# A windowed-attention block and a gated FFN on one core: another start, scales made on GpSimd, identity products ahead of the first FFN, and a new order of steps

## What is computed

```python
x = x + layernorm(attn(layernorm(x)))
x = x + layernorm(ffn(layernorm(x)))
```

```python
gate = silu((x @ w_gate) * s_gate)
up   = (x @ w_up) * s_up
out  = ((gate * up) @ w_down) * s_down
```

## Time and profile before

| quantity | value |
|---|---|
| median of 3 runs | 1000.24 us (999.96 to 1001.12) |
| the profiled execution's own time | 1001.03 us |
| its span, first to last instruction | 999.3 us |
| busy share of PE, DVE, POOL, ACT | 91%, 83%, 77%, 66% |
| mean granted TensorE clock | 0.968 of 2.4 GHz |

### The profile page before, as it was taken

How to read it: one execution, slowest core, us unless ns; L and a number is a source line. 1 busy time by engine, 2 the same in 40 slices (tenths; PEclk the granted TensorE clock), 3 DMA queues, 4 the chain that set the end, 5 groups by cost and what they waited for, 6 DMA issues and landing times.

```text
span 999.3 us, 17730 instructions
## 1 busy us (share of the span) xinstructions
PE 910.1 (91%) x6511; PEld 705.6 (71%) x6511; DVE 825.5 (83%) x1099; ACT 658.6 (66%) x1153; POOL 765.8 (77%) x698
## 2 busy tenths in 40 slices
PE   1566499989999999999999999999999999989996
PEld 1444387767878777777777787877777787767674
DVE  2799898978898998989898998989898989894322
ACT  1876477676768768586767778586767686654431
POOL 1477686978889797989889797988899787876432
PEclk9878599999999999999999999999999999989998
DMA  7112212040311313040402213040403111120201
GB/s 202 42 43 50 76 26 60 1 128 1 87 41 44 85 22 106 1 127 1 98 30 62 66 33 95 2 128 1 127 1 77 31 43 43 23 64 19 67 11 32
DMA packets 68886, 54.94 MB, mean 55 GB/s; under 512 B 40384, under 2 KB 56768, under 8 KB 68800
## 3 DMA queue, kind: packets, MB, share of 16 engines
q1 hardware_dynamic: 63936, 53.49, 20.0%
q10 hardware_dynamic: 4864, 0.32, 0.3%
HBM read 37.02 MB, written 16.78 MB: 54 GB/s over the span
## 4 chain that ended last, share of the span: by engine, by line
PE 76%; DVE 10%; POOL 5%; issue 3%; DMA 2%; ACT 2%; SPq 1%; POOLq 0%; DVEq 0%; ACTq 0%
PE ps_up L552 21%; PE ps_gate L552 19%; PE ps_acc L571 18%; PE ps_w L513 10%; PE ps_w L533 3%; PE ps_w L504 2%; POOL sum L808 2%; DVE fst L1033 2%; DVE xr L1028 2%; PE ps_w L543 2%; DVE prod L950 1%; PE ps_w L522 1%; DMA xrow<-in_L_attn_x 1%; DVE mid L1049 1%; SPq L432 1%
## 5 line engine op out<-in xcount | busy, mean ns | idle before, releaser
L808 POOL TENSOR_TENSOR sum<-prod 128x1024 f32<-128x1024 f32 x128 | 301.7, 2366 | 46.4 <-DVE prod L950 39.2
L950 DVE TENSOR_TENSOR prod<-ps_x,qkvl 128x2048 f32<-128x2048 f32 x128 | 291.3, 2279 | 5.0 <-ACT ps_x L664 4.6
L571 PE MATMUL ps_acc<-wd,mid 128*128 128x512 f16 x1024 | 241.4, 379 | 0.0
L552 PE MATMUL ps_gate<-xhi,wg 128*128 128x256 f16 x1024 | 233.6, 275 | 3.0 <-DVE xlo L1040 3.0
L552 PE MATMUL ps_up<-xhi,wu 128*128 128x256 f16 x1024 | 232.3, 274 | 1.6 <-DVE mid L1049 1.6
L552 PE MATMUL ps_gate<-xlo,wg 128*128 128x256 f16 x1024 | 233.6, 275 | 0.0
L552 PE MATMUL ps_up<-xlo,wu 128*128 128x256 f16 x1024 | 232.1, 274 | 0.0
L732 ACT ACTIVATE mid<-ps_gate,sgate 128x256 f32<-128x256 f32 x256 | 107.1, 470 | 170.0 <-PE ps_gate L552 169.5
L876 POOL TENSOR_TENSOR mid<-mid 128x512 f16<-128x512 f32 x128 | 148.7, 1162 | 52.4 <-ACT mid L738 52.4
L1049 DVE SCALAR_TENSOR_TENSOR mid<-ps_up,sup,mid 128x256 f32<-128x256 f32 x256 | 110.1, 471 | 91.2 <-PE ps_up L552 69.2
L571 PEld LDWEIGHTS ps_acc<-wd,mid 128*128 128x128 f16 x1024 | 100.3, 98 | 96.7
(11 more groups left out here) (138 smaller groups left out, 1279.6 us busy)
## 6 DMA issues: line engine op xcount, KB each, us to landing
xrow<-in_L_attn_x SPq DMA_DIRECT2D x16, 512.0 KB, 4.5
xb<-in_L_attn_x SPq DMA_DIRECT2D x128, 64.0 KB
attn_rows<-ratt SPq DMA_DIRECT2D x32, 256.0 KB, 2.6
o<-attn_rows SPq DMA_DIRECT2D x32, 256.0 KB, 3.5
xr<-in_L_attn_x SPq DMA_DIRECT2D x16, 512.0 KB, 5.0
out_x<-y SPq DMA_DIRECT2D x15, 512.0 KB, 5.3
mid<-in_L_ffn_w_gate SPq DMA_DIRECT2D x1, 1024.0 KB, 5.4
mid<-in_L_ffn_w_up SPq DMA_DIRECT2D x1, 1024.0 KB, 8.1
```

The lines of the kernel that those rows point to most:

```text
L552: mm = nc.tensor.matmul(ps[:, ROWS * i:ROWS * i + ROWS], w[:, k, P * j:P * j + P], xs[:, n % 2, k, :], start=(k == 0 and part == 0), stop= ...
L571: return nc.tensor.matmul(ps_acc[q][:], f[:, m % SPLITS, ROWS * i + P * q:ROWS * i + P * q + P], wd[:, 2 * m + i, :], start=(m == 0 and pa ...
L808: nc.gpsimd.tensor_tensor(sum4[:, u % 2, :].rearrange("p (s c) -> p s c", c=4), s[:, :, 0:4], s[:, :, 4:8], ALU.add).then_inc(half_done, 1)
L950: nc.vector.tensor_tensor(prod[:, half].rearrange("p (s j k) -> p s j k", j=WIN, k=WIN), left[:, :, None, :].broadcast_to([P, 4 * WIN, WIN ...
```

## The change

1. The start. `START` is a new list. SP loads the first slice's rows and its `xb` before anything else, then rows and `xb` of the next slices, and the FFN weights (`load_weights`) only after `xb` of slice 2. The casts stand later in it. It holds more of the attention than before: all of slice 1's `pv_sum`, all of slice 2's `qkv`, two of its `qk`, and two `xt` of slice 3.
2. The scales. GpSimd multiplies `sup`, `sgate` and `sdown` and splits the bias; VectorE keeps a copy, a reciprocal and one add. `proj` waits for `bias_split` now, and the first `fuse` of VectorE for `scales_set`.
3. `warm_fx`. Behind the `fx` transposes of slice 0 TensorE makes eight products of the identity with itself into `ps_acc1`, which nobody reads. The function was in the file before and no list named it.
4. The order. `PLAN` and `OWN` have other numbers: in the steady part the attention of a slice stands up to a slice earlier, `norm1_add` 6.4 slots ahead of its slice's gate in place of 3.6, and `spread` at another place. ScalarE's copy of the statistics now also waits until it has applied enough of the slice before (one `need` line).

```diff
-        START = [("cast", 0, 0), ("taps", 0), ("stats", 0), ("masks", 0), ("spread", 0), ("blocks", 0),
...
+        START = [("taps", 0), ("masks", 0), ("load_row", 0), ("stats", 0), ("blocks", 0), ("load_xb", 0),
...
+                 ("fx", 0, 1), ("qk", 2, 1), ("apply", 4), ("warm_fx", 0)]
-        PLAN = [(-109.09, ("load_row",)), (-93.33, ("load_xb",)), (-91.14, ("stats",)), (-74.78, ("spread",)),
...
+        PLAN = [(-150.00, ("load_row",)), (-119.88, ("stats",)), (-108.21, ("load_xb",)), (-106.52, ("spread",)),
...
@@ TensorE
             def proj(n, u, bank):
                 if n == 0 and u == 0:
-                    pe.wait_ge(scales_set, 1)
+                    pe.wait_ge(bias_split, 1)
@@ ScalarE, spread_stats
+                need(act, xn_done, WIN * n - WIN // 2)
@@ GpSimd
+            def scales(n, bank):
+                pool.wait_ge(brest_done, 1)
+                for i in range(3):
+                    third = slice(32 * i, 32 * i + 32)
+                    nc.gpsimd.tensor_copy(term[:], brest[:]).then_inc(terms_done, 1)
+                    pool.wait_ge(terms_done, 3 * i + 1)
+                    a = nc.gpsimd.tensor_copy(bterm[third], term[third])
+                    if i < 2:
+                        a.then_inc(terms_done, 1)
+                        pool.wait_ge(terms_done, 3 * i + 2)
+                        nc.gpsimd.tensor_tensor(brest[:], brest[:], term[:], ALU.subtract).then_inc(terms_done, 1)
+                        pool.wait_ge(terms_done, 3 * i + 3)
+                a.then_inc(bias_split, 1)
+                pool.wait_ge(bias_split, 1)
+                pool.wait_ge(top_both, 1)
+                nc.gpsimd.tensor_scalar(sup[:], sup[:], top[:, 4:5], 2.0 ** -18 / XSCALE, ALU.mult, ALU.mult)
+                nc.gpsimd.tensor_scalar(sgate[:], sgate[:], 1.0 / XSCALE, None, ALU.mult)
+                nc.gpsimd.tensor_scalar(sdown[:], sdown[:], top[:, 3:4], 2.0 ** 18, ALU.mult,
+                                        ALU.mult).then_inc(scales_set, 1)
@@ VectorE, fuse_step
+                if n == 0 and m == 0:
+                    dve.wait_ge(scales_set, 1)
@@ VectorE, scales: the fourteen instructions become these
                 link(nc.vector.tensor_copy(top[:, 3:4], ps_up[:, 0:1]))
+                nc.vector.reciprocal(top[:, 4:5], top[:, 3:4]).then_inc(top_both, 1)
                 dve.wait_ge(bias_done, 1)
+                nc.vector.tensor_tensor(brest[:], pbias[:], ps_gate[:, P:P + C], ALU.add).then_inc(brest_done, 1)
```

More of the change, by code:

```diff
@@ L163, in sandwich_kernel @@
         top_all = sem("top_all")
+        top_both = sem("top_both")
+        brest_done = sem("brest_done")
+        terms_done = sem("terms_done")
+        bias_split = sem("bias_split")
         scales_set = sem("scales_set")
@@ L373, in order @@
                     step = (name, n, *rest)
-                    if step not in placed and not (n == TILES - 1 and name in ("finish", "finish_apply", "finish_add")):
+                    if step not in placed and runs(name, n):
                         put(3 * CHUNKS * n + place, step)
@@ L900, in _ @@
                                     pattern=[[C, WIN + 2]], channel_multiplier=-1).then_inc(tokens_done, 1)
-            walk({"stats": stats, "token_bias": token_bias, "qk": qk, "pv": pv, "attn_out": attn_out,
+            walk({"stats": stats, "scales": scales, "token_bias": token_bias, "qk": qk, "pv": pv, "attn_out": attn_out,
                   "cent_out": cent_out, "ffn_norm1": ffn_norm1, "ffn_norm2": ffn_norm2, "finish": finish,
```

188 lines of the change are left out of this document (92 added, 96 removed), and 13 rows, old and new, of the table OWN.

## The result

| quantity | before | after |
|---|---|---|
| median | 1000.10 us (999.42 to 1001.12, 4 runs) | 983.05 us (981.15 to 984.48, 4 runs) |
| ratio, 95% interval | | 0.9827 (0.9806 to 0.9849) |
| profiled execution, its span | 1001.03, 999.3 us | 981.15, 979.4 us |
| first product of VectorE, first gate | 34.78, 117.32 us | 26.20, 110.64 us |
| busy share of PE, DVE, POOL, ACT | 91, 83, 77, 66% | 93, 88, 78, 67% |

The change made the kernel 17 us faster. Forecast were 27 (973.2 us): the time lies inside the range of 964 to 988, and right where the rival A had put it (984). So something ate 10 us, and the first place to look is the row of busy shares: VectorE was busy 825.5 us before and 863.2 after, though eleven of its fourteen scale steps had left it.

A forecast was written before the change was run, and what follows sets the result against it. TensorE bounds the steady middle; time is the first gate's moment plus TensorE's work and waits. Span 999.3 - 10.8 - 0.9 - 2.2 - 16.1 + 3 = 972.3 us, median 973.2 us, range 964 to 988.

The forecast's parts named there:

- rival A: After the first gate: start as worked out, old waits only half gained, new waits cost 6 us; 984 us, chance 0.2.
- from there to the end of the norms: First product to end of slice 0's second norm: VectorE's own work, 73.9 us against 75.8 before.
- GpSimd's eleven steps: Before the first gate: bias steps, two vectors and `sdown` moved to GpSimd take 3.5 us there.
- identity products: Ahead of the first gate: eight extra TensorE products delay it 1.9 us but raise the clock, 2.8 gained; net 0.9 gained.
- The start: Up to the first gate: earlier row loads and less VectorE work bring that gate 10.8 us earlier.
- 7.4 us for the scale steps: Before the first gate: moving scale steps off VectorE saves 7.4 of their 7.58 us there.
- The waits after the gate: TensorE's waits from 221.77 us to the last slice mostly go: 16.1 us gained, bounds 5 and 18.
- The 3 us for new waits: Steady slices: no TensorE wait in the mean slice, 3 us lost for those a little late, bounds 0 and 12.
- rival B: Start later than worked out, by constants, GpSimd's scale steps or casts, 4 to 7 us together; 978 us, chance 0.15.
- Rival C: Every slice: the hand-over of `xr` becomes the bound; 14 slices cost 49 us, 1018 us, slower than before; chance 0.05.
- The GpSimd form of B: Start: GpSimd's small steps each wait for VectorE's products, 21 us more; some 990 us, chance 0.03 of the 0.15.
- the signs named: Profile after: first product near 26 us, first gate 105 to 109, no `rmask` releaser after it, steady slices 55.2 us.

## Why the prediction was right, and where 10 us went

| step | predicted | measured |
|---|---|---|
| first product | 25.8 us | 26.20 |
| from there to the end of the norms | 73.9 | 76.1 (26.20 to 102.33) |
| first gate, behind the products | 108.4 | 110.64 |
| GpSimd's eleven steps | 3.5 | 3.54 (47.62 to 51.16) |
| identity products | 0.9 gained | 0.7 |
| slices 0 and 1 | 9.3 gained | 4.8 |
| slices 2 to 12 | 3.8 less 3, 0.8 gained | 1.7 lost |
| slices 13 and 14 | 8.0 gained | 10.1 |
| span | 972.3 | 979.4 |
| median | 973.2 | 983.05 |

**The start** was right in its first step, the load order, and in GpSimd's run. The stretch behind it was 2.2 us too short: `rmask` at 45.34 stood beside a halving for 1.88 us, and VectorE's waits came to 2.67 us (0.45, 1.01 and 1.21) in place of 1.76 before. Its largest term, 7.4 us for the scale steps, was a duration, not a gain. The runs put it at 2.1 to 2.6 us in the new order and at nothing in the old one. That the stretch was off by 2.2 us alone means that the rest of the new order won some 5 us that no term of the prediction has. That is luck, and I didn't take it apart further.

**The waits after the gate** hold the step that failed: "I get the sum held 1.1 us by `xr` on VectorE, and 1.3 to 1.6 us of room on TensorE". The walk gave the sum its 1.28 us of the earlier trace rows without a look at what GpSimd does beside it; in the old order that was nothing, in the new one two halvings. The 2.2 us more used up the room at `fx` and left 0.54 us of wait, which costs 0.92, in eleven slices and more in slice 9. With the sum in one instruction the program from the first gate on is 11.8 us shorter (857.0 in place of 868.8). That would be 7 us better than my 863.9. The 3 us for new waits weren't needed, and the eleven waits that went were worth about 0.35 us each more than their rows, which together is about that much. The prediction names, for rival B, the half of the rule in the Trainium skill, "SBUF — State Buffer", section "Who interferes with whom", that lets VectorE's products pass. The other half, two operands in SBUF, decides over the sum and `rmask`, and I applied it to neither. The slices 0 and 1 fell 4.5 us short. The single sum, which brings them to 106.0 us, accounts for 1.9 of that; a new wait of 0.76 us at 139.05 is another part, and the rest stays open. The slices 13 and 14 brought 2.1 more than forecast: the wait at 941.23, of which I had taken 0.7 off, went altogether.

**The rival A** had the size (984) by halving the gain from the old waits and adding 6 us of new ones. The first half didn't come, since the large waits went in full. The second did: in every steady slice the wait moved from `rmask` to `fx`, eleven times some 0.9 us. Its reason, an engine at 90%, isn't what was found. That the time came out within 1 us of its 984 is luck too. **Rival B** came in part: the first gate 2.2 us late. **Rival C** didn't come: `xr` was waited for twice, 0.40 and 0.67 us. **The GpSimd form of B** didn't either (3.54 us). Of the signs named, the first gate (105 to 109), the absence of `rmask` as a releaser and the steady slice of 55.2 us were missed; `rmask` beside a halving is in the first, and the slower slice pointed at the sum.

**The rest.** Of the 9.85 us between 973.2 and 983.05, 7.1 are the span, and 2.7 the profiled executions' places among their runs (0.8 above the median shown before the change, 1.9 below it after). Whether the clock in slice 9 has a part in that, no trace of the other three runs can tell.

## What to carry to other kernels

Before an instruction with two operands in SBUF is moved on VectorE, look at what GpSimd does at the new place, and price it with the wait; where such instructions stand in a row beside GpSimd work, make them one. A duration in a busy stretch is a gain only if nothing else arrives at the same time, and the engine that takes the work over must be free when it comes: the same steps were worth nothing in one order and some 2 us in the other. A change that makes the whole faster can still carry a loss in every slice, and the groups whose mean grew, at the same count and shape, show it at once.
